# A two-layer tower on one core: bias of the chosen expert by one matmul per pair, residual block inside the expert stage, another task order

## What is computed

```python
h = tokens(...)                                   # layer norm of a ternary linear map of six embeddings
h = h + linear_attention(layernorm(h))            # layer 0
h = h + ffn0(layernorm(h))                        # layer 0, eight experts
h = h + softmax_attention(layernorm(h))           # layer 1, eight heads
h = h + ffn1(layernorm(h))                        # layer 1, four heads with four query experts

def ffn0(x):
    H = gelu(x @ W1 + b1)                         # 256 hidden
    probs = softmax(H @ Wg + bg)
    e = argmax(probs)
    return probs[e] * (H @ Wd[e] + bd[e])         # one expert for each token

def ffn1(x):
    sx = x @ hl_w + hl_b                          # per head n, D = 16
    out = causal_softmax(q(sx) @ k(sx)) @ v(sx)   # four query experts per head
    mixed = gate(out) * out
    resid = sx[arange(4), arange(4)]              # batches 0 to 3, head n of batch n
    hn = layernorm(mixed + resid)
    ...                                           # two small layers, a norm, a gate
```

## Time and profile before

| | |
|---|---|
| median of 3 runs | 5210.67 us (5208.51 to 5212.81) |
| the profiled execution, its own time | 5214.04 us |
| its span, first to last instruction | 5212.3 us |
| PE busy | 4750.9 us (91%) |
| DVE busy | 3764.4 us (72%) |
| ACT busy | 3155.7 us (61%) |
| POOL busy | 2190.3 us (42%) |
| mean granted TensorE clock | 0.947 of full |

### The profile page before, as it was taken

One profiled execution on the slowest core, in us unless ns is written; L12 is line 12 of the kernel. 1 busy time (PEld: TensorE's weight loads), 2 busy tenths in 40 slices (PEclk: granted clock), 3 DMA queues, 4 the chain that ended last, 5 costly groups with the idle time before them and its releaser, 6 DMA issues. The chain is left out here.

```text
span 5212.3 us, 121968 instructions
## 1 busy us (share of the span) xinstructions
PE 4750.9 (91%) x42013; PEld 2134.6 (41%) x42013; DVE 3764.4 (72%) x6372; ACT 3155.7 (61%) x3388; POOL 2190.3 (42%) x2124
## 2 busy tenths in 40 slices
PE   4887787999999999999999979999999999999965
PEld 2333332333333333333333334444444444444433
DVE  5666665666666666666666658888888888888878
ACT  2322322666666666666666627788878788788854
POOL 2122123333333333333333325666666656666656
PEclk8888887999999999999999979999999999999976
DMA  4111100000000000000000000000000000000001
GB/s 112 33 48 48 48 16 0 2 2 1 2 1 2 2 1 2 2 2 1 2 2 2 1 1 2 3 3 3 3 3 3 3 3 3 3 3 3 3 5 28
DMA packets 43525, 52.95 MB, mean 10 GB/s; under 512 B 33164, under 2 KB 33295, under 8 KB 42896
## 3 DMA queue, kind: packets, MB, share of 16 engines
q1 hardware_dynamic: 39160, 44.34, 3.2%
q10 hardware_dynamic: 3736, 0.38, 0.1%
HBM read 39.70 MB, written 4.19 MB: 8 GB/s over the span
## 5 line engine op out<-in xcount | busy, mean ns | idle before, releaser
L1582 DVE TENSOR_REDUCE a_mp<-psum 128x1 f32<-128x512 f32 x2072 | 1324.7, 685 | 680.9 <-PE psum L1459 676.3
L2231 DVE TENSOR_REDUCE f_mp<-psum 128x1 f32<-128x512 f32 (+2 forms) x2352 | 1469.2, 682 | 238.3 <-PE psum L2075 157.2
L1427 ACT ACTIVATE a_prob<-psum,escale 128x1024 f32<-128x1024 f32 x1024 | 1087.9, 1111 | 535.7 <-PE psum L1508 535.4
L2035 ACT ACTIVATE f_prob<-psum,escale_f 128x1024 f32<-128x1024 f32 x1152 | 1238.5, 1112 | 236.7 <-PE psum L2152 147.8
L1516 PE MATMUL psum<-a_prob,a_v 128*64 128x512 f32 x4104 | 997.1, 607 | 0.0
L2075 PE MATMUL psum<-f_kf,f_qf 64*128 64x512 f16 (+2 forms) x3660 | 673.5, 309 | 51.0 <-issue 22.1
L1923 POOL TENSOR_SCALAR f_hi<-f_raw,part 128x512 f16<-128x512 f32 x320 | 500.7, 1565 | 441.3 <-ACT f_raw L2000 441.3
L1347 POOL TENSOR_TENSOR a_u<-a_og,a_inv 128x512 f32<-128x512 f32 x129 | 134.5, 1043 | 1166.7 <-DVE a_inv L1597 1166.7
L2165 PE MATMUL psum<-f_prob,f_vh 128*32 128x512 f32 (+3 forms) x6144 | 614.7, 495 | 7.2 <-DVE f_oc L2253 4.6
L2144 PE MATMUL psum<-f_qf,f_kf 64*128 64x512 f16 (+3 forms) x3074 | 498.9, 329 | 21.1 <-ACT f_og L2005 18.2
L1516 PEld LDWEIGHTS psum<-a_prob,a_v 128*64 128x64 f32 x4104 | 249.7, 136 | 508.5 <-issue 503.2
(11 more groups left out here) (428 smaller groups left out, 6983.6 us busy)
## 6 DMA issues: line engine op xcount, KB each, us to landing
idx<-in_itok_BS_dram SPq DMA_DIRECT2D x36, 512.0 KB, 6.0
idx<-in_itok_BS_dram SPq DMA_DIRECT2D x54, 256.0 KB, 6.8
idx<-in_x_dram SPq DMA_DIRECT2D x18, 256.0 KB, 3.8
a_qh<-a_rowT SPq DMA_DIRECT2D x258, 1.0 KB
out_dram<-h SPq DMA_DIRECT2D x16, 256.0 KB, 2.6
f_qf<-f_rowT SPq DMA_DIRECT2D x130, 4.0 KB, 1.7
wd<-in_L_ffn_Wd_dram SPq DMA_DIRECT2D x2, 256.0 KB
aw<-in_L_attn_WQ_dram SPq DMA_DIRECT2D x2, 128.0 KB
```

The lines of the kernel that those rows point to most:

```text
L1427: act.activation(prob[:, part], k.psum[:, pair:pair + 2].rearrange("p b n -> p (b n)"), ACT.Exp, scale=k.escale[:]).then_inc(s.read, 1)
L1582: dve.tensor_reduce(mp[:, tg % 2, t + 4 * r, c:c + 1], bank_of(j + r), X, ALU.max)\
L2035: act.activation(prob[:, u % NPF], k.psum[:, pair:pair + 2], ACT.Exp, scale=k.escale_f[:])\
L2231: dve.tensor_reduce(side[:, at[0]:at[-1] + 1:step], bank_of(j + r)[:, 0:len(at) * width].rearrange("p (a b) -> p a b", b=width), X, ALU.ma ...
```

## The change

1. **setup.** The row `bd1`, its split and the DMA to `bd3` go. Sixteen loads put `bd` (8 rows of 64) sixteen times below each other into `bd16`; POOL spreads it to `k.bias` (128 x 2 x 512) and cuts it with eight `affine_select` to blocks, so that row (tile, expert) holds that expert's bias in the columns of that tile.
2. **layer0.** The third matmul of each expert tile goes. `turn` goes from slot 2. In slot 3 PE transposes the 128 x 128 weights `wsel` (`weights_turn`), ACT copies them (`wT`), and behind tile 0 `residual` makes, for each batch, one 128 x 512 matmul of `wT` with `bias` and four 128 x 128 matmuls of `x2` with the identity into the same bank; ACT's copy to `xt` moves to slot 3.
3. **residual1** goes as a block. Its work stands in the start part of `feedforward1`: POOL normalizes after its own start work, PE's two transpose groups stand behind max tasks 1 and 2 and its two products behind tasks 4 and 6, two batches at a time (128 rows), and ACT copies. POOL, not DVE, splits the two q parts of the second group.
4. **The order in feedforward1** as the diff shows.

```diff
--- before.py
+++ after.py
+    loads += [(k.bd16[n * EXPERTS:(n + 1) * EXPERTS], a["bd"]) for n in range(2 * T)]
...
-            need(sp, "bd3", "consts")
-            sp.dma_start(k.bd3[0:3], k.bds[0:1]).then_inc(rows_in, 16)
-            sp.wait_ge(rows_in, 16)
...
+            for j in range(2):
+                blocks = k.bias[:, j].rearrange("p (t a c) -> p a t c", t=4, a=2)
+                signal(pool.tensor_copy(blocks, k.bd16[:].unsqueeze(1).unsqueeze(1).to_broadcast([P, 2, 4, C])), f"spread{j}")
...
+                for a in range(2):
...
+                    signal(pool.affine_select(out=here, in_=here, pattern=[[-EXPERTS, 4], [0, C]], compare_op=ALU.is_ge,
...
+                    if n == 3 and back is not None:
+                        done("wturn", back + 1)
+                        act.activation(wT[:], ps[7][:, 0:P], ACT.Copy).then_inc(E["wT"], 1)
...
+                def weights_turn(pair):
+
+                    done("wsel", pair + 1)
+                    pe.transpose(ps[7][:, 0:P], wsel[:].rearrange("p j t e -> p (j t e)"), k.ident[:]).then_inc(E["wturn"], 1)
+
+                def residual(pair):
+
+                    done("wT", pair + 1)
+                    for j in range(2):
+                        pe.matmul(ps[3 + 2 * j], lhsT=wT[:], rhs=k.bias[:, j], start=True, stop=False, skip_group_check=True)
+                        for t in range(4):
+                            last = pe.matmul(ps[3 + 2 * j][:, t * P:(t + 1) * P], lhsT=x2[:, j, t * P:(t + 1) * P], rhs=k.ident[:],
+                                             start=False, stop=True, skip_group_check=True)
+                        last.then_inc(E["tr"], 1)
...
-                    pe.matmul(bank, lhsT=k.onesb[:], rhs=k.bd3[:], start=False, stop=True).then_inc(E["y"], 1)
...
-                        if n == 2:
-                            for j in range(2):
-                                turn(back, j)
+                        if n == 3:
+                            weights_turn(back)
                         for tile in L_TILES[n]:
                             experts(back, tile)
+                            if tile == 0:
+                                residual(back)
...
-F_SUM_AT = (3, 6, 6, 9, 10, 11, 13, 15, 16, 17)
-F_PIECES = (((0, 0, 128, 0), (2, 256, 128, 128), (4, 512, 128, 256), (6, 768, 128, 384)), ((1, 0, 256, 0), (2, 0, 256, 256)), ((6, 0, 512, 0),), ((5, 0, 512, 0),), ((3, 0, 512, 0),), ((7, 0, 512, 0),), ((4, 0, 512, 0),), ((5, 512, 256, 0), (6, 512, 256, 256)), ((7, 512, 512, 0),))
+F_SUM_AT = (4, 7, 7, 9, 10, 12, 14, 15, 16, 17)
+F_PIECES = (
+    ((0, 0, 128, 0), (2, 256, 128, 128), (4, 512, 128, 256), (6, 768, 128, 384)),
+    ((5, 0, 512, 0),),
+    ((6, 0, 512, 0),),
+    ((7, 512, 512, 0),),
+    ((3, 0, 512, 0),),
+    ((7, 0, 512, 0),),
+    ((1, 0, 256, 0), (2, 0, 256, 256)),
+    ((4, 0, 512, 0),),
+    ((5, 512, 256, 0), (6, 512, 256, 256)),
+)
...
-F_ORDER = ('MS', '0S1', '0S1', 'MSV', 'SM', 'SM', 'SMV', 'SM', '0S1', 'MVS', 'MSV', 'MSV', 'MS', '0S1V', 'MS', 'SMV', 'MSV', 'MSV')
+F_ORDER = ('SM', 'S01', '0S1', 'MS', 'VMS', 'SM', 'SM', 'VSM', 'S01', 'VMS', 'SMV', 'SM', 'VMS', '0S1', 'V0S1', '0S1V', 'MSV', 'SMV')
...
-F_EXTRA = {1: (('k', 2, 0),), 2: (('q', 2, 0),), 5: (('out', -1, 0),), 8: (('q', 2, 1), ('x', 0, 0), ('s', 0, 0), ('s', 0, 1)), 10: (('v', 0, 0),)}
+F_EXTRA = {1: (('k', 2, 0),), 2: (('q', 2, 0),), 5: (('out', -1, 0),), 8: (('q', 2, 1),), 10: (('x', 0, 0), ('s', 0, 0), ('s', 0, 1)), 13: (('v', 0, 0),)}
...
+                residual_weights()
+                for n in range(NH):
+                    residual_tokens(n)
+                passed(pool, k.seen, s.laid, n_kq(0, 0, "q", 1, 1))
+                for n, (kind, of, part) in enumerate(F_START_STREAM):
+                    if kind == "q" and of == 1:
+                        split(0, of, kind, part, n + 1)
...
-                                if part == 7:
+                                if part == 4:
                                     logits(m, n2)
-                                if part == 12:
+                                if part == 13:
                                     mixture(m, i * 2 + x // 4 - (x % 4 == 0), n2)
...
+                for a in range(2):
+                    act.wait_ge(res.turned, a + 1)
+                    act.activation(res.xT[:, a], k.psum[:, 2 * a:2 * a + 2].rearrange("p b n -> p (b n)"), ACT.Copy).then_inc(res.copied, 1)
...
-                            if x % 2 == 0 and u == 12:
+                            if x % 2 == 0 and u == 13:
...
+                    if n in (1, 2):
+                        residual_turn(n - 1)
+                    if n in (4, 6):
+                        residual_product(n // 2 - 2)
+                pe.wait_ge(res.done, 2)
...
-                    elif kind in ("k", "q"):
+                    elif kind in ("k", "q") and of == 0:
                         first_split(n, of, kind, part)
...
-                                if u == 8:
+                                if u == 5:
                                     inverses(m, n2, n_stream(i, x, "out", 0))
...
-        residual1(k, nc)
         feedforward1(k, nc)
```

More of the change, by code:

```diff
@@ L911, in gates_turn @@
                     last.then_inc(E["gturn"], 1)
[L913 to L917, removed]
-                    last.then_inc(E["tr"], 1)
+                def weights_turn(pair):
[9 more added lines that the diff above has]
+                        last.then_inc(E["tr"], 1)
                 def experts(pair, n):
@@ L1027, in weighed @@
                     link(dve.tensor_tensor(e, e, wide(g1[:, 3], EXPERTS), ALU.mult))
-                    link(dve.tensor_tensor(w, w, e, ALU.mult))
+                    dve.tensor_tensor(w, w, e, ALU.mult).then_inc(E["wsel"], 1)
+                    done("wsel", pair + 1)
                 def outputs(pair, n):
@@ L1111, in _ @@
                 start = link.n
-                steps = start + 18
+                steps = start + 17
                 with dve.Fori(0, PAIRS_ - 1) as i:
@@ L2022, in _ @@
                     read_out(0, -1, kind, of + 1, part, 2 * (n % 2))
+                for a in range(2):
+                    act.wait_ge(res.turned, a + 1)
+                    act.activation(res.xT[:, a], k.psum[:, 2 * a:2 * a + 2].rearrange("p b n -> p (b n)"), ACT.Copy).then_inc(res.copied, 1)
+                for a in range(2):
+                    act.wait_ge(res.product, a + 1)
+                    act.activation(k.resid[:, :, 2 * a:2 * a + 2].rearrange("p t n d -> p t (n d)"),
+                                   ps[2 * a][:, 0:T * 2 * D].rearrange("p (t x) -> p t x", t=T), ACT.Copy).then_inc(res.done, 1)
                 act.wait_ge(s.blank, 4)
@@ L2169, in values, with residual_turn, residual_product @@
                     last.then_inc(s.pv, 1)
+                def residual_turn(a):
+                    pe.wait_ge(s.read, SS)
+                    pe.wait_ge(res.ready, 4 + 2 * a)
+                    for t in range(T):
+                        last = pe.transpose(ps[2 * a + t // 4][:, (t % 4) * P:(t % 4 + 1) * P],
+                                            res.x[:, a, t].rearrange("p s c -> p (s c)"), k.ident[:])
+                    last.then_inc(res.turned, 1)
+                def residual_product(a):
+                    pe.wait_ge(res.copied, a + 1)
+                    for t in range(T):
+                        last = pe.matmul(ps[2 * a][:, t * 2 * D:(t + 1) * 2 * D], lhsT=res.xT[:, a, t * P:(t + 1) * P],
+                                         rhs=res.w[:, a], start=(t == 0), stop=True, skip_group_check=True)
+                    last.then_inc(res.product, 1)
                 pe.matmul(ps[F_SUM], lhsT=k.ones[:], rhs=k.ones[:, 0:1].to_broadcast([P, HALF]), start=True, stop=True)\
```

112 lines of the change are left out of this document (41 added, 71 removed).

## The result

The changed kernel takes 5134.97 us (median of 4 runs, 5132.24 to 5141.02); the kernel before, on the same chip, 5211.74 us (5208.51 to 5213.6). The ratio is 0.9854, with a 95% interval of 0.984 to 0.9867: 77 us less, against 44 forecast.

A forecast was written before the change was run, and what follows sets the result against it. The prediction took PE to bound the kernel overall, with DVE close behind in the last attention's loop and pacing parts of layer 0. +2.5 - 14.7 + 4.5 - 26.5 - 10 = -44.2 us gave 5166 us, range 5130 to 5200.

The forecast's parts named there:

- Setup: Setup: more loads +2 us, POOL's later bias work +0.5; +2.5 us in all, bounds 0 and +6.7.
- Layer 0, the loop's pairs: Seven pairs of layer 0: ten tiles on PE's path save 0.21 us each, 2.1 a pair, 14.7 in all.
- rival 2: Layer 0, clock: projections behind slot 3 run at the upper level, -13 us more, 5153; chance 0.05.
- Slot 3: Layer 0, slot 3: added PE work fits its idle time, identity matmuls cost as transposes; 0 us, bound +1 a pair.
- Last pair: Layer 0's last pair: new chain unhidden, 6.5 us later, 14 tiles save 2; net +4.5 us, bounds +3.5 and +6.5.
- Residual block: Between the attentions: block goes -30.0, DVE's q splits -4.5, DVE's waits +8.0; -26.5 us, bounds -34.5 and -23.5.
- The order: Last attention's loop: new order of slots gains 10 us, bounds -77 and +56.
- v in slot 13: Last attention's loop: v moved from slot 10 gains up to half its 1.92 us of PE, 16 x 1.0 = -16.
- The inverse in slot 5: Last attention's loop: DVE's inverse (0.54 us, 32 times) moves in front of maxima PE waits for; +10 us.
- The bound: Last attention's loop: the most the order could gain is all PE's idle time there, -77 us.
- Rival 3: Last attention's loop: S before M in slots 0 and 1 delays DVE's banks; +56 us, 5232; chance 0.09 slower.
- rival 1: Last attention's loop: PE's idle time goes nearly whole, -60 us instead of -10, 5116; chance 0.08.

The follow-up runs named there:

- old_order: The changed kernel with the order in the last attention's loop taken back, setup, layer 0 and residual as changed: 5167.91 us, ratio 0.992 to the kernel before.
- the letters alone: The kernel before with only the new `F_ORDER` and `F_SUM_AT` (order of the slots' letters, the sums' slots): 5215.46 us, ratio 1.0006.
- the items alone: The kernel before with only the extra items moved (x and s from slot 8 to 10, v from 10 to 13): 5232.89 us, ratio 1.0043.
- all but the items: The changed kernel with the extra items in their old slots (x, s in 8, v in 10): 5170.43 us, ratio 0.9916 to the kernel before.
- fill_two_places: The changed kernel with tile 14's matmuls run four times and tile 0's also run twice early in slot 2: 5133.14 us, ratio 0.9852 to the kernel before.
- third_matmul: The changed kernel with a third matmul, of ones and zeros, in each expert tile again: 5183.65 us, ratio 0.9942 to the kernel before.

## Why the prediction was right, and where it failed

**Setup** was right in kind, too large in size. DVE's wait for the loads ended 1.1 us later, not 2. POOL's work on the bias takes 4.8 us (40.81 to 45.56) and not the 7.1 that I had worked out; before it was 4.3, and the half microsecond cost nothing:

```profile
38.95 1.75 DVE L489 TENSOR_TENSOR aw<-aw 64x1536 f32<-64x1536 f32 x1 [23.18 <-DMA mgate<-in_L_ffn_gate_w_dram]
```

**Layer 0, the loop's pairs.** The count of ten tiles, their 0.21 us and the two places where the gain is lost were right; PE's wait before the last tile is still 6.59 us. What the sum lacked is the clock: rival 2 saw one place (slot 4, 1.9 us a pair) and gave it 0.05. In fact it came in three of six pairs, 3.9 us each (2.1 at the hidden layer, 1.8 in slots 3 and 4), and the other three lost 1.5 us each: with ten tiles in six pairs that is 12.6 + 11.7 - 4.5, the 19.8 us measured. The term was -14.7 and the stretch measured -21.1, its seven pairs -24.3.

**Slot 3.** I set sixteen f32 instructions against eight transposes and found them the same. That step was wrong: the transposes' row (1.92 us in the earlier trace rows) was at the lower level of the clock, and the row that I priced the identity matmuls by (2.0 us for sixteen) at the upper. At the upper level after, four transposes are busy for 0.60 us and four blocks by identity for 1.05; by the distance between two starts a block costs 0.11 us as a transpose and 0.22 by identity:

```profile
242.13 0.60 PE L910 MATMUL psum<-ident,l_gT 128*128 128x128 f32 x4
...
255.17 0.33 PE L916 MATMUL psum<-ident,l_wsel 128*128 128x128 f32 x1 [1.35 <-DVE l_wsel L1037]
255.34 1.88 PE L939 MATMUL psum<-wd,l_hT 128*128 128x512 f32 x4
257.06 1.02 PE L922 MATMUL psum<-bias,l_wT 128*128 128x512 f32 x2
257.91 1.05 PE L924 MATMUL psum<-ident,l_x 128*128 128x128 f32 x8
```

So the rule of the Trainium skill (Perfetto Trace Analysis, section Transposes), to do logical transposes as transposes, is borne out for f32: half the time. Here that is 0.9 us a pair for eight blocks, in PE's idle time, where it costs nothing, as forecast. Whether a transpose could add to the bias that stands in the bank, as the identity matmul does here, no run shows.

**Last pair.** +4.3 against +4.5, and part of that is luck. The weights were ready 1.6 us earlier in the pair, since more of the hidden layer ran at the upper level. From there to DVE's second product it took 10.6 us against 1.7 before, 8.9 more and not 6.5, since PE had waited and made tile 0 and the first bias matmul at the lower level (3.62 and 1.92 us). The 14 tiles then saved 2.9, and not 2:

```profile
793.01 3.62 PE L939 MATMUL psum<-wd,l_hT 128*128 128x512 f32 x4
...
796.73 0.69 DVE L1046 TENSOR_TENSOR l_yw<-psum,l_wsel 128x512 f32<-128x512 f32 x1 [4.04 <-PE psum L939]
...
802.97 0.69 DVE L1046 TENSOR_TENSOR l_yw<-psum,l_wsel 128x512 f32<-128x512 f32 x1 [5.55 <-PE psum L939]
```

**Residual block.** -26.5 as forecast, of three terms: -30.0 for the block; -3.2 instead of -4.5 for the splits (first instruction to first maxima: 27.4 us before, 24.2 after); +6.7 instead of +8.0 for DVE's waits (1.34, 0.86, 1.38 and 3.00 us). The two small errors cancelled; the one in the waits is that the first product ran mostly at the upper level. No experiment took this part by itself; it rests on the two traces and on `old_order`, where it stands with the same 65 us.

**The order** is the step that failed: -38.5, not -10. Over the whole loop a group takes 28.34 us; 1852.3 - 10 us in 64 groups would be 28.8 (I had written 28.7). So by the mark that I had set (0.4 us a group) the prediction is wrong in this step, though the time is inside its range: the range let the loop gain up to 45 us, and no term of my sum leads to 38. My list of what changes was also short: S and M change places in slots 4 and 11 too. Four of its parts:
- v in slot 13. I had 16 us. The time in which its instructions let PE start nothing else fell from 30.8 to 24.8 us in the loop, 6 us, but moved in the old order the items made the kernel 22 us slower. The price of a matmul in its old slot says nothing on what its new slot does to the banks.
- The inverse in slot 5. I wrote +10, since it would leave "a place where DVE waits anyway". The timeline above shows DVE without a pause from before the inverse to 3 us behind it. DVE's work is on the path in both slots, so the move itself costs nothing; what I left out is what hangs on it, POOL's logits and DVE's step behind them. With the other helpers' slots it gains about 6 us.
- PE's waits for maxima, forecast to halve (-4). The ones that are shown grew from 8.9 us to 20.2, while the kernel got faster. The table of PE's waits in the loop after (us, times, longest):

```profile
PE psum L2140 <- DVE f_mp L2318: 20.2, 92, 0.4
```

- The bound. I took PE's idle time, 77 us, and its short waits as all that an order can give back. The idle time stayed, and the gain came from waits inside busy rows. Starts would have shown that there are such waits (0.63 us in place of 0.21 in the row above, 64 times, though that one by itself was worth nothing). DVE's idle time would have been a bound with room in it: 263 us before, of which 29 went; with 9 us less of DVE's work that is the 38 us.

Rival 3 (S before M in slots 0 and 1 starves DVE) did not come; rival 1 named the direction of the loop's gain, but by the idle time, which didn't move.

**What stays open.** Why letters and items pay only together isn't settled. In the groups with x DVE does the same 24 us of work in all kernels, and waits for PE 4.16 us before, 4.20 with the letters alone, 4.77 with the items alone, 4.25 with all but the items and 3.64 after. So it is DVE's waits that shrink only with both; which of PE's items makes which of them I did not isolate. Whether the helpers' new slots would gain 0.5 us with the old letters too was not tried, nor each of the four by itself, nor was the residual's work at another place of the start part.

## What to carry to other kernels

On an engine that streams, judge an order by the distances between starts, not by its idle time: short waits hide under modelled ends. Then look at the idle time of the engine that takes its results: where DVE works without a pause here, no other order of PE's gained anything. A visible wait names where two engines meet, not what makes it; with another matmul in front of it the same wait of 0.4 us, 64 times, showed elsewhere and nothing was saved. Test parts of a schedule in both directions, from the old and from the new version, for parts that lose or give nothing alone (22 us slower, no change) may together make most of a gain of 38.

## What the runs showed of the hardware

- The last loop's step back to its begin costs about 4 us over an ordinary group (32.1 against 27.8 us, seven times), and that differs between kernels with the same loop code: 32.1 after, 33.2 in `fill_two_places`, 35.2 in `third_matmul`, where 3.1 us more, seven times, are 22 us. In `third_matmul` each of them has a second pause of PE of 1.6 to 2.4 us that waits for nothing shown. In these kernels only PE's instructions in layer 0, and constants in `third_matmul`, differ. I had not expected an edit in one stage to cost over 20 us in another; its cause is not settled.
- The granted clock can alternate between loop turns of the same work (pairs of 89.6 and 94.8 us, six in a row, the same in all six kernels with this layer 0), and taking 2 us of matmuls out of a pair moved it by more than they were worth in half of the pairs.
